# Cross attention on one core: gamma and variance loaded first, x ahead of theta and phi, batch 0's next context behind T, the last tile row stored in three pieces

## The reference, cut to what matters

```python
B, C, CI, N = (16, 512, 256, 1024)
g_x = conv1x1(g_w, g_b, x_2).transpose(0, 2, 1)
theta_x = conv1x1(theta_w, theta_b, x).transpose(0, 2, 1)
phi_x = conv1x1(phi_w, phi_b, x_2)
W = einsum('bnc,bcm->bnm', theta_x, phi_x) / phi_x.shape[-1]
y = einsum('bnm,bmc->bnc', W, g_x).transpose(0, 2, 1)
wy = conv1x1(w_w, w_b, y)
inv_std = rsqrt(bn_var + 1e-5)
wy = bn_gamma * (wy - bn_mean) * inv_std + bn_beta
out = wy + x
```

## Time and profile before

| | |
|---|---|
| median of 3 runs | 789.48 us (789.16 to 789.52) |
| profiled execution | 790.07 us |
| its span | 788.3 us |
| PE busy | 772.0 us |
| PEld busy | 666.7 us |
| POOL busy | 527.5 us |
| DVE busy | 498.1 us |
| ACT busy | 303.7 us |
| HBM read and written | 69.35 MB, 33.55 MB |

### The profile page before, as it was taken

The page is one execution under the profiler, slowest core; times in us unless marked ns, Lnnn a source line. Parts: engine busy times, 40 slices in busy tenths (PEclk is TensorE's granted clock), DMA queues, the critical chain, the costliest instruction groups (busy, mean ns, idle before and its releaser), DMA issues.

```text
span 788.3 us, 11592 instructions
## 1 busy us (share of the span) xinstructions
PE 772.0 (98%) x4045; PEld 666.7 (85%) x4045; DVE 498.1 (63%) x889; ACT 303.7 (39%) x514; POOL 527.5 (67%) x358
## 2 busy tenths in 40 slices
PE   4999999999999999999999999999999999999997
PEld 4688888888888888888888888888888888888886
DVE  3796574847657496574847657496574847657254
ACT  3634542325334243542325334243542325334131
POOL 4969785767857578585767857578585767857400
PEclk9999999999999999999999999999999999999999
DMA  9828254181733707255181733707255181730202
GB/s 237 197 108 214 107 129 192 35 226 62 178 142 74 246 0 213 106 124 195 33 228 58 178 142 72 247 0 213 106 121 198 32 228 60 178 143 1 107 1 106
DMA packets 55127, 103.17 MB, mean 131 GB/s; under 512 B 2474, under 2 KB 37956, under 8 KB 55108
## 3 DMA queue, kind: packets, MB, share of 16 engines
q1 hardware_dynamic: 52976, 101.86, 44.2%
q10 hardware_dynamic: 2132, 1.05, 0.8%
HBM read 69.35 MB, written 33.55 MB: 131 GB/s over the span
## 4 chain that ended last, share of the span: by engine, by line
PE 96%; DVE 1%; DMA 1%; ACT 1%; issue 0%; DVEq 0%; SPq 0%
PE wbank L667 57%; PE gbank L667 37%; PE wbank L830 1%; DMA ctx_sb<-in_ctx_dram 1%; PE wbank L708 1%; DVE x_sb L486 0%; PE wbank L686 0%; PE wbank L714 0%; ACT x_sb L366 0%; DVE tmp L509 0%; DVE tmp L508 0%; ACT x_hi L340 0%; DVE junk L590 0%; DVE x_sb L657 0%; DVE th_lo L583 0%
## 5 line engine op out<-in xcount | busy, mean ns | idle before, releaser
L286 POOL TENSOR_TENSOR ctxT_lo<-ctxT,ctxT_hi 128x512 fp32r<-128x512 f32 x124 | 167.2, 1349 | 205.7 <-ACT ctxT_hi L340 205.7
L297 POOL TENSOR_TENSOR ctx_sum<-ctx_sum,ctxT 128x512 f32<-128x512 f32 x108 | 157.0, 1454 | 0.2
L315 POOL TENSOR_TENSOR x_lo<-x_sb,x_hi 128x1024 fp32r<-128x1024 f32 x60 | 142.3, 2403 | 0.0
L340 ACT ACTIVATE mt<-wbank 128x512 fp32r<-128x512 f32 x64 | 37.9, 597 | 236.6 <-PE wbank L667 236.6
L657 DVE SCALAR_TENSOR_TENSOR x_sb<-wbank,const,x_sb 128x512 f32<-128x512 f32 x112 | 78.9, 747 | 73.1 <-PE wbank L667 73.1
L667 PE MATMUL wbank<-ctxT_lo,ctxT_hi 128*128 128x512 f32 x512 | 121.6, 393 | 0.0
L518 DVE TENSOR_TENSOR stage<-gbank,mt 128x384 f32<-128x384 f32 x64 | 28.3, 486 | 139.7 <-PE gbank L667 139.7
L667 PEld LDWEIGHTS wbank<-ctxT_lo,ctxT_hi 128*128 128x128 f32 x512 | 95.5, 190 | 18.7 <-POOL ctxT_lo L286 0.2
L340 ACT ACTIVATE ctxT_hi<-ctxT 128x512 fp32r<-128x512 f32 x124 | 76.5, 628 | 88.1 <-DVE ctxT L486 88.1
L667 PE MATMUL gbank<-ctxT_hi 128*128 128x384 f32 (+1 forms) x512 | 80.8, 314 | 10.1 <-ACT ctxT_hi L340 10.1
L667 PEld LDWEIGHTS gbank<-ctxT_hi 128*128 128x128 f32 x512 | 80.0, 191 | 12.0 <-issue 10.1
(11 more groups left out here) (107 smaller groups left out, 1327.4 us busy)
## 6 DMA issues: line engine op xcount, KB each, us to landing
x_sb<-in_x_dram SPq DMA_DIRECT2D x16, 2048.0 KB, 7.8
out_dram<-x_sb SPq DMA_DIRECT2D x64, 512.0 KB, 2.6
ctx_sb<-in_ctx_dram SPq DMA_DIRECT2D x60, 512.0 KB, 8.4
ctx_sb<-in_ctx_dram ACTq DMA_DIRECT2D x4, 256.0 KB, 7.1
ctx_sb<-in_ctx_dram SPq DMA_DIRECT2D x4, 256.0 KB, 7.2
x_sb<-in_L_xattn_w_w_dram SPq DMA_DIRECT2D x1, 512.0 KB, 11.7
stage<-in_L_xattn_theta_w_dram SPq DMA_DIRECT2D x1, 512.0 KB, 12.5
phi_nat<-in_L_xattn_phi_w_dram SPq DMA_DIRECT2D x1, 512.0 KB, 12.7
```

The costliest lines, as they stand in the source:

```text
L286: nc.gpsimd.tensor_tensor(ctxT_lo[:, c, :], turned_ctx(b, c), f(ctxT_hi[:, c, :]), ALU.subtract).then_inc(sem_, 1)
L297: nc.gpsimd.tensor_tensor(ctx_sum[:, :], ctx_sum[:, :], src, ALU.add).then_inc(ctxT_used, 1)
L315: nc.gpsimd.tensor_tensor(x_lo[:, k, :], x_sb[par][:, k, :], f(x_hi[:, k, :]), ALU.subtract).then_inc(x_lo_made, 1)
L340: nc.scalar.activation(dst, src, ACT.Copy).then_inc(sem_, 1)
```

## The change

**Start.** Gamma and variance get rows and a transpose of their own (`norm_rows` in a spare part of x_sb, `turn_norm`), and are the first loads of ScalarE's and SP's queue; VectorE works out the scale ahead of its first context transpose. SP loads parts 0 and 1 of the context, both halves in a row, and ScalarE parts 2 and 3. The other six vectors are loaded behind them and turned behind chunk 4's S matmuls, and VectorE copies them behind its eight transposes (`vec_taken`, a new semaphore; ScalarE's bias columns, `turn_w` and const now wait for it). x is loaded ahead of theta and phi. VectorE makes x_lo for the channel groups 0 and 1, GpSimd for 2 and 3.

**Batch 0's body.** `next_ctx()` on VectorE moves from ahead of theta(0) to behind `const`; on ScalarE `next_hi(0)` to `next_hi(3)` move from ahead of theta(0) to behind t_hi.

**End.** In the last batch the last row is made and stored in three pieces of 512, 256 and 256 columns, one after the other, each in a bank of its own (`LAST_PIECES`, `last_row`).

```diff
-            load_first_ctx(sp, (0, 2), 0)
-            load_vectors(sp, range(0, 4))
-            load_first_ctx(sp, (0, 2), 1)
+            sp.dma_start(norm_rows[KC:2 * KC, :], bn_var.rearrange("(m p) -> m p", p=P)).then_inc(in_norm, 16)
+            load_first_ctx(sp, (0, 1), 0)
+            load_first_ctx(sp, (0, 1), 1)
+            load_vectors(sp, range(0, 3))
             sp.dma_start(w_nat, w_w.rearrange("(m p) c -> p m c", p=P)).then_inc(in_w1, 16)
+            load_x(0, 0)
             sp.dma_start(theta_nat, theta_w.rearrange("(k p) c -> p k c", p=P)).then_inc(in_w4, 16)
             sp.dma_start(phi_nat[:, :, :], phi_w.rearrange("(k p) c -> p k c", p=P)).then_inc(in_w3, 16)
-            load_x(0, 0)
...
-                for m in range(KC):
+                for m in range(KC if nxt else KC - 1):
                     sp.wait_ge(work_free, NO * b + NH * (m + 1))
...
+                if not nxt:
+                    m = KC - 1
+                    for i, (a, n, bank) in enumerate(LAST_PIECES):
+                        sp.wait_ge(work_free, NO * b + (NH * m + i + 1))
+                        sp.dma_start(out[b].rearrange("(m p) n -> p m n", p=P)[:, m, a:a + n],
+                                     x_sb[par][:, m, a:a + n]).then_inc(stored, 16)
...
-            for k in range(1, KC):
+            for k in (2, 3):
                 pool.wait_ge(x_hi_made, k + 1)
...
-            load_first_ctx(act, (1, 3), 0)
-            load_vectors(act, range(4, 8))
-            load_first_ctx(act, (1, 3), 1)
+            act.dma_start(norm_rows[0:KC, :], bn_gamma.rearrange("(m p) -> m p", p=P)).then_inc(in_norm, 16)
+            load_first_ctx(act, (2, 3), 0)
             act.wait_ge(ident_done, 2)
             nc.scalar.activation(tmp[:, 7, :], ident[:, 0:KC], ACT.Sqrt)
+            load_first_ctx(act, (2, 3), 1)
+            act.wait_ge(vec_step, 1)
+            nc.scalar.activation(tmp[:, 1, :], tmp[:, 0, :], ACT.Sqrt).then_inc(root_done, 1)
+            load_vectors(act, range(3, 6))
...
             act.wait_ge(ones_done, 1)
+            act.wait_ge(vec_taken, 1)
             for k in range(KI):
...
-                if first(b):
-                    next_hi(0)
-                    next_hi(1)
-                    next_hi(2)
...
-                next_hi(3)
+                if not first(b):
+                    next_hi(3)
                 theta(0)
...
                 if first(b):
-                    next_hi(4)
-                    next_hi(5)
+                    for c in range(6):
+                        next_hi(c)
                 next_hi(6)
                 next_hi(7)
...
-            dve.wait_ge(in_first[0], 16 * QT)
-            for c in range(RING):
-                transpose_chunk(0, c)
-            dve.wait_ge(vec_turned, 1)
-            chain(nc.vector.tensor_copy(vec_cols[:, :], wbank[3][:, 0:5 * KC + 3 * KI]))
+            dve.wait_ge(norm_turned, 1)
             chain(nc.vector.tensor_scalar(ve, var_, EPS, None, ALU.add))
...
             nc.vector.tensor_scalar(scale[:, :], r0, 1.0 / N, None, ALU.mult).then_inc(scale_made, 1)
+            for h in range(2):
+                dve.wait_ge(in_first[h], 16 * QT)
+                for c in range(RING):
+                    transpose_chunk(0, h * RING + c)
+            dve.wait_ge(vec_turned, 1)
+            nc.vector.tensor_copy(vec_cols[:, :], VEC_BANK[:, 0:3 * KC + 3 * KI]).then_inc(vec_taken, 1)
...
             first_x_lo_part(0)
+            first_x_lo_part(1)
...
                 if first(b):
-                    next_ctx()
                     dve.wait_ge(in_bp, 16)
...
                     chain(nc.vector.tensor_tensor(const[:, :], r3, beta_, ALU.add))
+                    next_ctx()
                     transpose_chunk(b + 1, 4)
                     transpose_chunk(b + 1, 5)
...
+            def turn_norm():
+                pe.wait_ge(ident_done, 2)
+                pe.wait_ge(in_norm, 16 * 2)
+                nc.tensor.transpose(NORM_BANK[:, 0:2 * KC], norm_rows, ident[0:2 * KC, 0:2 * KC]).then_inc(norm_turned, 1)
+
...
-                        if c == 1:
+                        if c == RING:
                             turn_vectors()
...
+                def last_row(m):
+                    for a, n, bank in LAST_PIECES:
+                        if bank is OUT_BANK[1][0]:
+                            pe.wait_ge(work_free, NO * b + (NH + 1))
+                        for k in range(KI):
+                            q_h, q_l = q_hi[:, k, m * P:(m + 1) * P], q_lo[:, k, m * P:(m + 1) * P]
+                            mm(bank[:, 0:n], q_h, th_hi[:, k, a:a + n], k == 0, False)
+                            mm(bank[:, 0:n], q_h, th_lo[:, k, a:a + n], False, False)
+                            ins = mm(bank[:, 0:n], q_l, th_hi[:, k, a:a + n], False, k == KI - 1)
+                        ins.then_inc(out_done, 1)
```

More of the change, by code:

```diff
@@ L108, in xattn_kernel @@
         p1 = sb("p1", [P, KI])
-        vec_rows = sb("vec_rows", [5 * KC + 3 * KI, P])
-        vec_cols = sb("vec_cols", [P, 5 * KC + 3 * KI])
-        bt_col, bp_col, bg_col = (vec_cols[:, 5 * KC + i * KI:5 * KC + (i + 1) * KI] for i in range(3))
+        vec_rows = sb("vec_rows", [3 * KC + 3 * KI, P])
+        vec_cols = sb("vec_cols", [P, 3 * KC + 3 * KI])
+        bt_col, bp_col, bg_col = (vec_cols[:, 3 * KC + i * KI:3 * KC + (i + 1) * KI] for i in range(3))
         nbp_col = sb("nbp_col", [P, KI])
@@ L173, in xattn_kernel @@
         vec_step = sem("vec_step")
-        vec_turned = sem("vec_turned")
+        vec_turned, vec_taken = sem("vec_turned"), sem("vec_taken")
+        in_norm, norm_turned = sem("in_norm"), sem("norm_turned")
         root_done, scale_made = sem("root_done"), sem("scale_made")
@@ L487, in transpose_chunk @@
                                     ctx_sb[:, :, 32 * c:32 * c + 32]).then_inc(ctxT_made, 1)
[L489 removed]
+            wb_, beta_, mean_ = (vec_cols[:, i * KC:(i + 1) * KC] for i in range(3))
+            gamma_, var_ = NORM_BANK[:, 0:KC], NORM_BANK[:, KC:2 * KC]
             ve, root, r0, r2, r3, r4, wm = (tmp[:, i, :] for i in range(7))
[L492 to L496 removed]
+            dve.wait_ge(norm_turned, 1)
             chain(nc.vector.tensor_scalar(ve, var_, EPS, None, ALU.add))
[L498 to L499 removed]
             dve.wait_ge(root_done, 1)
             chain(nc.vector.reciprocal(r0, root))
[L502 removed]
             chain(nc.vector.tensor_tensor(r2, r0, r0, ALU.mult))
[L504 removed]
             chain(nc.vector.tensor_tensor(r3, r2, ve, ALU.mult))
[L506 removed]
             chain(nc.vector.tensor_scalar(r4, r3, -0.5, 1.5, ALU.mult, ALU.add))
@@ L628, in body @@
                 if first(b):
+                    dve.wait_ge(vec_taken, 1)
                     chain(nc.vector.tensor_tensor(wm, wb_, mean_, ALU.subtract))
@@ L652, in body @@
                 theta(1)
+                def last_row(m):
+                    for i, (a, n, bank) in enumerate(LAST_PIECES):
+                        dve.wait_ge(out_done, NO * b + (NH * m + i + 1))
+                        nc.vector.scalar_tensor_tensor(out=x_sb[par][:, m, a:a + n], in0=bank[:, 0:n],
+                                                       scalar=const[:, m:m + 1], in1=x_sb[par][:, m, a:a + n],
+                                                       op0=ALU.add, op1=ALU.add).then_inc(work_free, 1)
                 for m in range(KC):
+                    if m == KC - 1 and not nxt:
+                        last_row(m)
+                        break
                     for h in range(NH):
@@ L667, in mm @@
                 return nc.tensor.matmul(dst, lhsT, rhs, start=start, stop=stop, skip_group_check=True)
+            def turn_norm():
+                pe.wait_ge(ident_done, 2)
+                pe.wait_ge(in_norm, 16 * 2)
+                nc.tensor.transpose(NORM_BANK[:, 0:2 * KC], norm_rows, ident[0:2 * KC, 0:2 * KC]).then_inc(norm_turned, 1)
             def turn_vectors():
-                pe.wait_ge(ident_done, 2)
-                pe.wait_ge(in_vec, 16 * 8)
-                rows = 5 * KC + 3 * KI
-                nc.tensor.transpose(wbank[3][:, 0:rows], vec_rows[:, :], ident[0:rows, 0:rows]).then_inc(vec_turned, 1)
+                pe.wait_ge(in_vec, 16 * len(VECTORS))
+                pe.wait_ge(vec_step, 7)
+                rows = 3 * KC + 3 * KI
+                nc.tensor.transpose(VEC_BANK[:, 0:rows], vec_rows[:, :], ident[0:rows, 0:rows]).then_inc(vec_turned, 1)
             def turn_theta_phi():
@@ L693, in turn_w @@
                     if k == 0:
-                        pe.wait_ge(vec_step, 1)
+                        pe.wait_ge(vec_taken, 1)
                     else:
@@ L794, in theta @@
                             pe.wait_ge(low_lo_made, 2 * b + 2)
-                        if m == 0 and first(b) and k == 0:
+                        if m == 0 and first(b) and k < 2:
                             pe.wait_ge(first_x_lo, k + 1)
                         elif m == 0 and first(b):
```

(9 more changed lines are left out.)

15 lines of the change are left out of this document (7 added, 8 removed).

## The result

| | before | after |
|---|---|---|
| median | 789.62 us (6 runs, 789.16 to 790.80) | 794.12 us (6 runs, 793.72 to 794.57) |
| profiled execution | 790.07 us | 794.49 us |
| its span | 788.3 us | 792.6 us |

The changed kernel takes 1.0053 times as long, with a 95% interval from 1.0042 to 1.0063: 4.5 us slower. The forecast was 796.0 (range 792.8 to 798.0). Its direction came true, and so did its two largest terms, the wait and the slower clock. It was 1.9 us too high, nearly all of it in one term, the start. By the number alone the rival "the clock stays" (793.2) is nearer than the forecast, and 794.12 lies just outside the 794.6 to 797.5 that the forecast gave itself. What decides between them is the trace, further down: the clock did fall.

A forecast was written before the change was run, and what follows sets the result against it. TensorE was taken to bound the kernel, its chain 96% of the span, never waiting between 51 us and the last matmul. -0.9 - 0.73 + 6.6 + 2.8 - 1.3 = +6.5 us made 796.0 us on the median, range 792.8 to 798.0.

The forecast's parts named there:

- the wait: TensorE stands idle ahead of batch 0's first output matmul, on VectorE's q_lo: +6.6 us.
- the slower clock: Batch 0's output matmuls behind the idle gap run at the 1.2 GHz level: +2.8 us (ends 0 and 4).
- the start: Loads, first chunks and turning of w ahead of batch 0's body get shorter: -0.9 us (-1.3 to +0.3).
- the clock stays: Rival: TensorE stalls ahead of batch 0's output but then runs 2.2 columns per ns at once: 793.2 us, chance 0.14.
- wait in T: TensorE's wait in T of batch 0 goes, with ScalarE's 2.41 us of copies gone from ahead of theta(0): -0.73 us.
- last row, with all between: Last batch's end in three pieces: last operation 0.65 us sooner, landing 0.65 shorter; -1.3 us (-0.6 to -2.0).
- The next context behind const: Batch 0: first transpose 3.5 us after T, then GpSimd's four-place ring holds q; output starts 5.0 us later.
- The first loads: One small load ahead of the context on either queue: context 0.3 us later (ends 0 and 1.0).
- The first chunks: The other vectors' transpose moves from chunk 1 to chunk 4, where TensorE runs at the higher level: 0.15 us less.
- The 1.1 us wait: TensorE's wait at the turning of w, on ScalarE's first copy of M, goes: -1.05 us (ends 0 and -1.1).
- The start does not get shorter: Rival: x still lands late, vec_taken holds ScalarE, or the context comes 1 us later: 797.5 us, chance 0.12.
- The free gate: Rival: batch 0's ring wait is hidden in TensorE's q and theta(1) work: -2.9 us, 786.6 us, chance 0.08.

The follow-up runs named there:

- e3_filled: Changed kernel with 26 matmuls of 512 columns that nobody reads put ahead of batch 0's output on TensorE: 791.93 us, ratio 1.0026.
- e1: Changed kernel with batch 0's next context back ahead of theta(0) on VectorE and ScalarE; start and end of the change stay: 785.80 us, ratio 0.9941.
- e2: Kernel before with only the move of the next context behind const: 796.83 us, ratio 1.0085.
- e4: Changed kernel with chunks 4 to 7 of batch 1 moved from ahead of q's combination to behind theta(1): 785.10 us, ratio 0.9931.
- e5: Kernel before with only the last row in three pieces: 788.47 us, ratio 0.9980.
- e7: Kernel of e1 with x loaded behind theta and phi again: 786.36 us, ratio 0.9956.
- e8: Kernel of e1 with SP's three vector loads back between its two context halves: 785.56 us, ratio 0.9938.
- e6: Kernel of e1 with the context's first load dealt out as before, parts 0 and 2 from SP, 1 and 3 from ScalarE: 786.64 us, ratio 0.9952.
- e9: Kernel of e4 with 60 unread matmuls of 128 columns on TensorE ahead of the first chunk: 790.72 us.

## Why the prediction was right, and where it was off

The steps on the profiled executions, before against after; each is the difference between two points on TensorE's timeline:

| step | predicted | measured | how |
|---|---|---|---|
| start, to batch 0's column sums | -0.9 | -2.76 | 45.40 to 42.64 |
| wait in T | -0.73 | -1.0 | from there to the output's readiness: 18.10 to 17.11 |
| wait at the output | +6.6 | +6.5 | 59.75 to 66.22 |
| slower clock | +2.8 | +2.9 | 24 matmuls: 5.60 to 8.52 |
| last row, with all between | -1.3 | -1.34 | from batch 0's third output row to the span's end: 719.20 to 717.86 |
| sum | +6.5 | +4.3 | spans 788.3 and 792.6 |

(17.11 is from e3_filled, where the filling matmuls at 59.22 show the moment at which TensorE is ready.)

- **The next context behind const** was right in mechanism and size. The first transpose was forecast 3.5 us after T's end and came 52.56 - 49.03 = 3.5 after it, and from it to q_lo 13.6 us (13.8 forecast). In the 3.5 lay a step without a reason: they were measured from VectorE's last T operation, and that had begun 1.6 us after T's end before (54.39 against 52.75). The prediction let it begin at T's end. It did, at 49.05: with GpSimd idle VectorE's t_lo of one block took 0.42 us instead of 1.55 and 1.12, so it kept up. With the old lag the wait would have been some 8.1 us, by estimate. e1 and e2 show that the move alone makes the wait; the VectorE rows and e4 show that it is the ring and not the number of operations. One t_lo before, and one in the changed kernel:

```profile
51.48 1.55 DVE L609 TENSOR_TENSOR mt<-stage,mt 128x256 fp32r<-128x256 f32 x1
```

```profile
48.01 0.42 DVE L619 TENSOR_TENSOR mt<-stage,mt 128x256 fp32r<-128x256 f32 x1
```
- **The clock** fell as taken, and the price read off the start was right to 0.1 us in the profiled execution of the changed kernel. That close a fit is luck. Its mean granted clock was 0.993, the other five executions had 0.995 or 0.996, and e2's profiled one, with 0.996, paid 1.7 us; on the medians e3 lies 2.2 us below the changed kernel. e3 shows the clock as a cost of its own. The Trainium skill's rule on idle gaps between bursts of matmuls (TensorE: Matmul & The Clock Gate, section "Why this matters for your kernels") agrees with the trace: 0.50 after the gap, 1.00 throughout where the gap was filled. The gaps that the rule names are longer than the 1.95 us behind which e5's clock had fallen; there the measurement decides.
- **The start** is the term that failed: -0.9 forecast with ends -1.3 and +0.3, -2.76 measured. Two of its parts are behind it, the first loads with 1.2 us and the first chunks with 0.5.
- **The first loads.** I had the first half of the context 0.3 us later, because a small load stands ahead of it; it landed 0.92 us sooner (first chunk at 9.21, not 10.13). I priced the load that was added and gave the new order of parts and vectors no price at all; 0.0 to 1.0 us later was my range, which excluded a gain without a reason. The cause stays open: with the order of before, e5 had the first chunk at 9.46, so up to 0.7 us of the gain can be the execution.
- **The first chunks** took 5.47 us to the third one instead of 6.16. My term was -0.15 for the vectors' transpose. Its move gained nothing: it was 0.30 us long in chunk 1, and chunk 4, where it stands now, took 1.88 us (17.72 to 19.60) against 1.52 for its neighbours. The rest is the length of the slow stretch, which differs from trace to trace (below).
- **The 1.1 us wait** went, -1.04 measured on the stretch from the third chunk to the turning of theta (11.38 to 10.34), -1.05 forecast. The fit is two things that cancel: from the turning of w to that of theta it is 2.26 to 0.88 us, 1.4 less, and the vectors' transpose in chunk 4 takes back 0.34. And of the two causes that I named, the early x wasn't needed (e7). What the early x is worth isn't clear of the noise (786.36 against 785.80, with intervals that overlap); its trace shows a wait of 0.7 us.
- **The wait in T**: 1.0 us came back instead of 0.73. With the context in its old place it was 0.4 in e1, and 0.4 also in e5, which has the start of before; so its size differs from trace to trace.
- **The last row**: from the first matmul of the last row (781.11 before, 786.59 now) to the end of the last operation it took 4.11 and 3.47 us, 0.64 less, and from there to the span's end 3.08 and 2.54 us, 0.54 less. Forecast were 0.65 and 0.65, so the row itself gave 1.18; the other 0.16 of the table lies in the batches between, where nothing was changed. e5 gives 1.4 us on the median.

Of the rivals, "the clock stays" (793.2) is refuted by the windows at 0.50 and by e3, not by the time: had the start gained only what was forecast, the same wait and clock would have made about 796. "The start does not get shorter" is refuted by its 2.76 us. The free gate (786.6) comes true when chunks 4 to 7 don't stand in front of q: e4_ring_split, 785.1, with the longer gain at the start.

## What to carry to other kernels

When work is moved behind a milestone, follow the ring it goes through: a producer may be quick, and still wait place by place for the slowest consumer, whose work was hidden until then. Here 5 us of VectorE work became 11.5 us, and the engine that mattered was one that no line of the moved code names. Split such a run at the ring's size (e4_ring_split), and put only what fits into free places ahead of the critical operation; and price a gap on TensorE with the slower matmuls that follow it, or fill it.

## What the runs showed that I had not expected

- The slow stretch at the start has no fixed length. From the first to the third chunk it took 4.86 us (e3_filled), 5.24 (e5), 5.27 (e7), 5.34 (e8), 5.43 (e2), 5.47 (changed kernel), 5.92 (e1 and e4), 5.93 (e6) and 6.16 us (before), for the same matmuls but for the vectors' transpose of 0.24 to 0.30 us, which stands in it in e2, e5 and before. This alone puts more than 1 us between executions.
- The time of the kernel before varies with its mean granted clock: of the 21 executions beside e5, e6, e8 and e9, seven of the eight above 790.0 us had 0.997 or 0.998, and the thirteen below had 0.999 or more. Whether that is the fall of the clock at the turning of w that e5's trace shows isn't shown; the trace of the kernel before doesn't have it.
- The granted clock read 1.00 in the first chunks, although their matmuls ran at half the rate, and 0.50 in the gap of batch 0, where it agreed with their rate. At the start the lengths of the matmuls are the better witness.
- Sixty matmuls of 128 columns ran 0.218 us apart, and 13 us of them did not bring the chunk behind them to the higher level; fourteen of 512 columns in 6.1 us did.
- These fourteen, which compute nothing that is used, made e4_ring_split 1.4 us faster.
